# A fused language tower on one core: Gram products for two groups of four positions in column halves, two positions a transfer, later normalisers, first expert chunk inside the last step

## The chip, the cores and the metric

The kernel runs on one core of one Trainium2 chip. The metric is the device time of one execution in microseconds (us). The kernel before takes 741.24 us in the median of 3 runs (737.28 to 750.5). What can be told from no change is about 2% of that, 15 us.

## The reference

The input is 16 x 128 token numbers. The reference applies five blocks to a residual stream `h` of shape (16, 128, 64):

```python
h = L0_tok(x)                              # embedding, decaying memory, 4 MLP layers of 128 -> 512 -> 128, head to 64
h = h + L0_attn(layernorm(h))              # fast weights, described below
h = h + L0_ffn(layernorm(h))               # 8 experts 64 -> 128 -> 64, routed by the mean over 128 positions
h = h + L1_attn(layernorm(h))              # attention of 8 heads with positional scores
h = h + L1_ffn(layernorm(h))               # 8 experts, top 2 for each row
```

The change is in the second and third block. `L0_attn` runs over the first axis: 16 steps, for 128 positions and 8 heads of width 32, with a state of 32 x 32 per head:

```python
q, k = sum_norm(elu(q) + 1), sum_norm(elu(k) + 1);  rk = softmax(rk)
v_old = W @ k_t;   W = W + beta * (v_t - v_old) k_t^T;   z_t = W @ q_t
r_old = R @ rk_t;  R = R + rbeta * (rv_t - r_old) rk_t^T;  h_t = z_t + R @ softmax(h_{t-1})
out_t = x_t + concat(h_t) @ out_W^T
```

`L0_ffn` takes the mean of the normalised rows over the 128 positions of each of the 16 steps, two softmaxes of the router's logits with a capacity scale between them, the two largest weights, and the weighted sum of the experts.

## The kernel before, in words

Everything lies in the on-chip memory, with the 128 positions on the partitions; `t` is the step (T = 16), a chunk is CH = 4 steps, NC = 4 chunks.

**The Gram stage.** The kernel never builds the 32 x 32 states. It keeps for each step the updated value rows (`UV`), and needs inner products of every step's key or query with every earlier step's key. These are Gram products over (step, position), of which only those with equal position are wanted. The features stand transposed in `feat[0..5]` (32 rows for each of four heads on the 128 partitions). `grams(g)` takes a group of GB = 8 positions: for 8 heads and KD = 3 kinds one product of 16 x 8 = 128 columns of weights by 17 x 8 = 136 moving columns (the 17th step is a row of ones, whose products are the sums to divide by). There are NG = 16 groups; the heads of k = 0 go to banks 0 to 3, those of k = 1 to banks 4 to 7. ScalarE and VectorE copy two banks each of a half to a staging buffer (128 x 408 values a bank), of which there are NS = 4. Of each block of 8 x 8 positions only the diagonal is wanted. `relay(eng, g, j)` is a transfer from one place of the chip's memory to another: it reads 16 partitions (the 16 steps of position j of the group), 408 values each, and writes them side by side into the one partition `16 * j + g` of `C`. Three of a group's eight transfers are issued by the sync engine SP (lines 405 to 409), five by GpSimd (lines 574 to 579; of the last group two by ScalarE). Before a staging buffer is written again, `relayed` waits until its eight transfers have landed.

**Normalisers.** When all transfers have landed, VectorE's `row_sums` and `sums` (lines 1707 to 1722) invert the sums, make the strengths `bsum`, `bsum2` and scale the query coefficients, first for steps 0 to 3, then for steps 4 to 15, before `next_query(0)`.

**The steps.** `step(t)` on VectorE (line 1800) makes the softmax of the state, the read coefficients, the products of the `rec` kind, adds the output of step t - 1 to `H`, and then calls `next_query(t + 1)`, whose `update` gives GpSimd and TensorE what they need for the next step (`held`, `queries`, lines 493 to 520). TensorE (lines 1264 to 1275) sums and turns the products; ScalarE evicts (lines 825 to 834).

**The way out of the steps.** In step 15 VectorE makes the statistics and the normalised rows of chunks 0 to 2 (lines 1807 to 1812), with the inverse roots from GpSimd (`rstd_pool`, line 335); chunk 3 follows at lines 1902 to 1904. TensorE sums the columns (`means`), turns chunk 0 (`turn_x(0, 0)`), and the router's small softmaxes go to and fro between VectorE, ScalarE and TensorE (lines 1345 to 1361, 1939 to 1971), while ScalarE makes the Gelus of chunk 0 between the router's exponentials (lines 863 to 867). Then follow the bias products, `expert_up(0, 1)`, `turn_x(0, 2)` and the first `expert_down(0, 0)` (lines 1362 to 1370). VectorE's positional scores (lines 2005 to 2018) stand before its first addition of expert results (line 2024).

The order of the work on each engine is the order in which it is written; engines wait for each other by counted semaphores.

## Time and profile before

| what | value |
|---|---|
| median of 3 runs (lowest to highest) | 741.24 us (737.28 to 750.5) |
| the profiled execution | 740.56 us |
| its span | 738.7 us, 12304 instructions |
| busy: TensorE, its weight loads, VectorE | 606.3, 477.8, 445.8 us |
| busy: ScalarE, GpSimd | 280.9, 360.0 us |
| chain that ended last, by engine | PE 55%, DVE 26%, ACT 7%, DMA 4%, issue 4%, POOL 3% |
| DMA packets | 10699, 10.35 MB |
| DMA queue 0 (from GpSimd), queue 1 (from SP) | 2496 packets 2.04 MB, 7424 packets 7.12 MB |
| mean granted TensorE clock | 0.91 |

The profile is of one execution. Its page gives the busy time of each engine, the span in 40 equal slices, the DMA queues, the chain of waits that ended last, and the costliest groups of instructions by line. PE is TensorE, PEld its weight loads, DVE VectorE, ACT ScalarE, POOL GpSimd, SPq the sync engine's queue. A row `L1127 PE MATMUL bank<-features 32*128 32x136 f32 x768` is line 1127, weights of 32 rows by 128 columns, 136 moving columns, 768 times; an fp32 product is two such instructions. The square brackets of a timeline row hold the engine's idle time before it and what ended that.

### The profile page before, as it was taken

The page shows a single profiled execution, that of the slowest core. Times are in us where ns is not written, and L with a number is a line of the kernel's source. Part 1 is how long each engine was busy: PE and PEld are TensorE (multiplying, and loading weights), DVE is VectorE, ACT ScalarE, POOL GpSimd, SP SyncE. Part 2 cuts the span into 40 slices and gives each one's busy share as a digit, 9 for nine tenths or more (in the row PEclk, how much of TensorE's full clock was granted, in tenths as well). Part 3 has the DMA queues.
Part 4 walks back from the last instruction along what each step waited for, and adds up shares of the span by engine and source line. Part 5 has one row for each costly group of instructions (what it writes and reads, how often), then busy time and mean ns, then how long its engine had stood idle before and what let it go on. Part 6 is the DMA issues. An engine that isn't in the chain of part 4 may idle for free.

```text
span 738.7 us, 12304 instructions
## 1 busy us (share of the span) xinstructions
PE 606.3 (82%) x4657; PEld 477.8 (65%) x4657; DVE 445.8 (60%) x1113; ACT 280.9 (38%) x502; POOL 360.0 (49%) x414
## 2 busy tenths in 40 slices
PE   6889999999987707788877888456999698899996
PEld 3657777785556606677776777352678487785776
DVE  3643444236667756787899999952553736663533
ACT  0075453528966602111110000006553337566550
POOL 1696333218018836797899998143463300001334
PEclk9999999999989956888999999755999869999999
DMA  7000000000004450000000000000000000000000
GB/s 242 1 1 1 2 1 1 0 1 1 0 10 75 78 88 4 1 1 1 1 1 1 1 1 1 0 1 0 1 1 1 1 1 2 1 2 1 8 8 14
DMA packets 10699, 10.35 MB, mean 14 GB/s; under 512 B 5905, under 2 KB 9681, under 8 KB 10385
## 3 DMA queue, kind: packets, MB, share of 16 engines
q1 hardware_dynamic: 7424, 7.12, 3.6%
q0 software_dynamic: 2496, 2.04, 2.0%
q8 instruction: 37, 0.61, 0.4%
q10 hardware_dynamic: 720, 0.41, 0.3%
q14 instruction: 22, 0.17, 0.1%
HBM read 5.70 MB, written 0.52 MB: 8 GB/s over the span
## 4 chain that ended last, share of the span: by engine, by line
PE 55%; DVE 26%; ACT 7%; DMA 4%; issue 4%; POOL 3%; SPq 0%; ACTq 0%; DVEq 0%; POOLq 0%
PE bank L1059 8%; PE bank L1047 7%; DVE features L1743 6%; DVE bank L1777 5%; DVE features L1766 5%; PE bank L1315 4%; PE bank L1136 4%; PE bank L1333 4%; PE bank L1331 4%; PE bank L1403 2%; PE bank L1096 2%; PE bank L1391 2%; PE bank L1127 2%; PE bank L1105 2%; DMA RK<-in_wf 1%
## 5 line engine op out<-in xcount | busy, mean ns | idle before, releaser
L1136 PE MATMUL bank<-ident,features 128*128 128x128 f32 x920 | 126.9, 297 | 63.1 <-DVE features L1743 39.3
L1136 PEld LDWEIGHTS bank<-ident,features 128*128 128x128 f32 x920 | 113.8, 155 | 73.4 <-DVE features L1743 48.0
L506 POOL TENSOR_TENSOR features<-UV,coefs 128x1024 f32<-128x1024 f32 (+1 forms) x64 | 117.6, 1864 | 25.7 <-DVE UV L1730 12.5
L1743 DVE TENSOR_TENSOR features<-UV,bank 128x1024 f32<-128x1024 f32 (+3 forms) x64 | 66.2, 1066 | 0.9
L685 ACT ACTIVATE G<-bank,cols 128x512 f32<-128x512 f32 x64 | 43.3, 687 | 49.5 <-PE bank L1047 49.5
L1047 PE MATMUL bank<-xs,weights 128*128 128x512 f32 x128 | 60.2, 615 | 2.3 <-ACT xs L676 2.3
L1059 PE MATMUL bank<-weights,G 128*128 128x128 f32 x512 | 59.8, 275 | 0.0
L1059 PEld LDWEIGHTS bank<-weights,G 128*128 128x128 f32 x512 | 58.4, 192 | 0.0
L349 POOL TENSOR_SCALAR rstd<-mv 128x4 f32<-128x4 f32 x8 | 1.9, 238 | 112.2 <-DVE mv L361 112.2
L752 ACT ACTIVATE hsT<-bank 128x256 f32<-128x256 f32 x16 | 6.2, 385 | 102.3 <-PE bank L1136 102.3
L1127 PE MATMUL bank<-features 32*128 32x136 f32 x768 | 34.8, 320 | 10.5 <-DVE G L1703 4.1
L481 POOL TENSOR_TENSOR UV<-xs,rows 128x512 f32<-128x512 f32 x16 | 20.3, 1271 | 46.7 <-DVE xs L1652 46.6
L1766 DVE TENSOR_TENSOR features<-RK,bank 128x1024 f32<-128x1024 f32 (+3 forms) x40 | 41.8, 1044 | 0.1
L1047 PEld LDWEIGHTS bank<-xs,weights 128*128 128x128 f32 x128 | 24.0, 198 | 27.4 <-issue 24.5
L1777 DVE TENSOR_REDUCE bank<-features 128x32 f32<-128x1024 f32 (+3 forms) x40 | 41.5, 1056 | 0.0
L1127 PEld LDWEIGHTS bank<-features 32*128 32x128 f32 x768 | 29.7, 212 | 15.6 <-ACT G L736 4.6
L340 POOL TENSOR_SCALAR rstd<-mv 128x4 f32<-128x4 f32 x32 | 7.7, 241 | 61.8 <-DVE mv L361 60.6
L2065 DVE TENSOR_REDUCE RK<-bank 128x4 f32<-128x512 f32 x32 | 21.9, 684 | 26.0 <-PE bank L1391 26.0
L1652 DVE TENSOR_TENSOR xs<-bank,UV 128x512 f32<-128x512 f32 x16 | 11.1, 692 | 40.9 <-PE bank L1059 38.0
L342 POOL TENSOR_TENSOR rstd<-rstd,neghalf 128x4 f32<-128x4 f32 x32 | 33.2, 1038 | 2.7
L652 POOL TENSOR_TENSOR features<-features 128x512 f32<-128x512 f32 (+2 forms) x21 | 17.2, 818 | 27.1 <-DVE features L2158 17.1
L614 POOL TENSOR_TENSOR features<-weights,RK 128x512 f32<-128x512 f32 x16 | 16.4, 1043 | 28.0 <-PE bank L1331 15.6
(312 smaller groups left out, 1350.6 us busy)
## 6 DMA issues: line engine op xcount, KB each, us to landing
weights<-in_w SPq DMA_DIRECT2D x2, 1024.0 KB, 11.8
features<-in_tok SPq DMA_DIRECT2D x1, 768.0 KB, 6.3
weights<-in_ew SPq DMA_DIRECT2D x4, 128.0 KB, 3.0
weights<-in_ew SPq DMA_DIRECT2D x2, 256.0 KB, 2.9
coefs<-G POOLq DMA_DIRECT2D x20, 25.5 KB, 3.9
coefs<-xs POOLq DMA_DIRECT2D x20, 25.5 KB, 5.2
coefs<-weights POOLq DMA_DIRECT2D x20, 25.5 KB, 5.3
coefs<-sx POOLq DMA_DIRECT2D x18, 25.5 KB, 5.0
```

Of the source, the lines that this page charges most:

```text
L342: pool.tensor_tensor(rstd[:, k, 0:n], rstd[:, k, 0:n], neghalf[:, 0:n], ALU.pow).then_inc(s["ln_rstd"], 1)
L506: pool.tensor_tensor(out, u, co, ALU.mult).then_inc(s["held_p"], 1)
L685: act.activation(G[:, 4 * (w % 2) + f, :], up_bank(f)[:], ACT.Gelu, bias=col("b1", 4 * i + f)).then_inc(s["tok_gelu"], 1)
L1047: mm(up_bank(f)[:], w1[:, i, P * f:P * f + P], xT[:, w % 2, :], start=True, stop=True).then_inc(s["tok_up"], 1)
L1059: last = mm(down_bank(w)[:, DT * j:DT * j + DT], G[:, 4 * (w % 2) + f, P * j:P * j + P], w2[:, i, f, :], start=(f == 0), stop=(f == 3))
L1127: last = mm(bank[4 * k + j][:, GB * SL * n:GB * SL * n + GB * SL], feat[left + k][x, g, 0:T].rearrange("p s b -> p (s b)"), feat[right + k ...
L1136: last = mm(out[:, P * k:P * k + P], x[:, P * k:P * k + P], ident[:], is_transpose=True, start=first and k == 0, stop=last_ and k == n - 1 ...
L1315: mm(expert_bank(k, c, e)[:], ew1[k][r, e // 2, :], xin(k, c)[r], start=True, stop=True).then_inc(s[f"x_up{e % 2}"], 1)
L1331: last = mm(bank[4 + t % 2][:, 0:D], g, w2w[:, t % NW, e, :], start=(e == 0), stop=(e == E - 1))
L1743: dve.tensor_tensor(out, u, co.unsqueeze(3).broadcast_to([P, R, NH, DH]), ALU.mult)\
L1766: ch(dve.tensor_tensor(PD[:, j, 0:R * HB].rearrange("p (r x) -> p r x", r=R), RK[:, r0:r1_, :], e.unsqueeze(1).broadcast_to([P, R, HB]), A ...
L1777: ch(dve.tensor_reduce(bankCR[:, r0:r1_, :], PD[:, j, 0:(r1_ - r0) * HB].rearrange("p (r h j) -> p r h j", r=r1_ - r0, h=NH), AX_X, ALU.add))
```

## The change

Groups have 4 positions (GB = 4, NG = 32) and are treated in pairs: NR = 16 rounds. In a round each product of before becomes two, of 64 weight columns by 68 moving columns, one for each group of the pair, into partitions 0 to 63 and 64 to 127 of the same bank. A bank's copy has 204 values a partition in place of 408. There are NS = 6 staging buffers of half the size, in three of the four tensors used before. A transfer reads 32 partitions and writes two neighbouring partitions, `32 * j + 2 * g` and the next one: four transfers a round in place of eight, two from SP and two from GpSimd, none from ScalarE.

```diff
-GB = 8
+GB = 4
+NR = NG // 2
-NS = 4
+NS = 6
...
-            b = NG * j + g
-            eng.dma_start(CF[b:b + 1, 0:T * ROWC].rearrange("p (t x) -> p t x", t=T),
-                          stage[g % NS][j:P:GB, j].rearrange("p c s -> p (c s)"))\
+            b, x = NG * j + 2 * g, g % NS
+            eng.dma_start(CF[b:b + 2, 0:T * ROWC].rearrange("p (t x) -> p t x", t=T),
+                          stage[x][j:P:GB, j].rearrange("p c s -> p (c s)"))\
...
-            for g in range(NG):
+            for g in range(NR):
                 sp.wait_ge(s["gram_act"], 4 * g + 4)
                 sp.wait_ge(s["gram_dve"], 4 * g + 4)
-                for j in range(0, 3):
+                for j in (0, 1):
                     relay(sp, g, j)
...
-                            last = mm(bank[4 * k + j][:, GB * SL * n:GB * SL * n + GB * SL],
-                                      feat[left + k][x, g, 0:T].rearrange("p s b -> p (s b)"),
-                                      feat[right + k][x, g].rearrange("p s b -> p (s b)"), start=True, stop=True)
+                            for h in range(2):
+                                last = mm(bank[4 * k + j][D * h:D * h + D, GB * SL * n:GB * SL * n + GB * SL],
+                                          feat[left + k][x, 2 * g + h, 0:T].rearrange("p s b -> p (s b)"),
+                                          feat[right + k][x, 2 * g + h].rearrange("p s b -> p (s b)"), start=True, stop=True)
```

`sums` is split: before `next_query(0)` only steps 0 to 3 are inverted (`normalisers`), get their strengths and their query coefficients scaled, and of these only the columns in use. The rest goes into steps 0 to 4, and the first statistics and normalised rows into steps 5 and 8:

```diff
-                if t == T - 1:
-
-                    for c in range(NC - 1):
-                        norm_stats(dve, ch, ("f0", c), [H[:, i, :] for i in range(CH * c, CH * c + CH)])
-                    for c in range(NC - 1):
-                        x_apply(c)
                 if t:
                     out_add(t - 1)
+                if t == CH + 1:
+                    x_stats(0)
+                if t == 2 * CH:
+                    x_apply(0)
+                if t == 0:
+                    normalisers(slice(CH, T))
+                if t == 1:
+                    ch.settle()
+                    strengths(slice(CH, T))
+                if t >= 2 and t + 2 < 2 * CH - 1:
+                    query_scale(t - 1)
                 if t + 1 < T:
                     next_query(t + 1)
...
             for t in range(T):
                 step(t)
+            x_stats(1)
+            x_stats(2)
+            x_apply(1)
             out_add(T - 1)
-
+            dve.wait_ge(s["o_add"], T)
+            x_stats(NC - 1)
+            x_apply(2)
+            x_apply(NC - 1)
```

GpSimd makes the inverse root of chunk 0 before `held(7)`. TensorE turns chunk 0 and makes its eight up products inside step 15, with banks 4 and 5 for them, and ScalarE its Gelus there; chunk 1 takes the place of chunk 0 beside the router, and `turn_x(0, 2)` comes before the router's last product:

```diff
                 queries(t)
+                if t == T - 1:
+                    pe.wait_ge(s["load_experts"], 16 * 17)
+                    pe.wait_ge(s["pad"], 2)
+                    turn_x(0, 0)
+                    expert_up(0, 0)
                 read_out("rec", t, reads_of("rec", t))
...
+                if t == T - 1:
+                    experts(0, 0)
+                    expert_gelus(0, 0)
+                state(t)
+
+            experts(0, 1)
             act.wait_ge(s["mean_mm"], 1)
             act.activation(meanT[:], bank[7][0:D, 0:T], ACT.Copy, scale=1.0 / P).then_inc(s["mean_ready"], 1)
-            experts(0, 0)
             for j in range(3):
                 act.wait_ge(s["r_sub"], j + 1)
                 act.activation(rsel[0:T, j, :], rsel[0:T, j, :], ACT.Exp).then_inc(s["r_exp"], 1)
-                expert_gelus(0, 0, 2 * j, 2 * j + 2)
-            expert_gelus(0, 0, 6, E)
+            expert_gelus(0, 1, 0, 4)
             act.wait_ge(s["wT_mm"], 1)
             act.activation(wtsT[:], bank[7][:, 256:384], ACT.Copy).then_inc(s["wT_ready"], 1)
-            experts(0, 1)
+            expert_gelus(0, 1, 4, E)
+            experts(0, 2)
...
             pe.wait_ge(s["hs_saved"], T)
-            for c in range(NC - 1):
+            out_projection(T - 1)
+            means(0)
+            turn_x(0, 1)
+            for c in range(1, NC):
                 means(c)
-            out_projection(T - 1)
-            means(NC - 1)
+            expert_up(0, 1, 0, 2)
...
-            expert_up(0, 0, 0, 2)
+            pe.wait_ge(s["o_add"], T)
+            expert_up(0, 1, 2, 4)
             pe.wait_ge(s["r_prob"], 1)
...
-            expert_up(0, 0, 2, 6)
+            turn_x(0, 2)
             pe.wait_ge(s["r_spread"], 1)
...
-            turn_x(0, 1)
             bias(0)
+            expert_up(0, 1, 4, E)
```

## Rows read from the trace of the kernel before

**Rows 1.** Busy time by stretch: Gram stage, steps, way out to the expert chunks.

```profile
core 0: us, PE busy (x) PEld busy (x) DVE busy (x) ACT busy (x) POOL busy (x), PEclk, DMA share, GB/s
214.20:269.00 54.80, 34.78 (x768) 29.67 (x768) 33.38 (x65) 28.79 (x64) 37.65 (x78) 0.84 0.44 63
276.00:481.50 205.50, 155.09 (x1158) 139.93 (x1159) 176.83 (x252) 24.94 (x60) 162.21 (x108) 0.89 0.01 1
481.50:526.00 44.50, 29.57 (x134) 17.93 (x132) 21.46 (x104) 18.78 (x29) 16.75 (x20) 0.68 0.00 1
```

**Rows 2.** Groups by line in the Gram stage: busy us, mean ns, idle before.

```profile
L1703 DVE COPY xs<-bank 128x408 f32<-128x408 f32 x16 | 8.4, 577 | 3.9 <-PE bank L1127 2.3 <-DMA coefs<-xs 1.6
```

**Rows 3.** Timeline of SP's queue: the first two transfers.

```profile
218.54 1.18 SPq L379 DMA_DIRECT2D coefs<-G  x2
```

**Rows 4.** Busy time by stretch again: transfers in two fillings of queues, and weight loads.

```profile
224.00:226.00 2.00, 1.85 (x48) 1.48 (x48) 1.78 (x4) 1.44 (x4) 2.00 (x5) 1.00 0.58 92
...
262.00:264.00 2.00, 0.00 (x0) 0.00 (x0) 0.00 (x0) 0.00 (x0) 0.00 (x0) 0.50 1.06 72
272.00:282.00 10.00, 3.91 (x17) 3.15 (x17) 6.76 (x14) 1.07 (x3) 4.75 (x7) 0.50 0.34 89
```

**Rows 5.** The chain of waits in order of time: start, length, what.

```profile
221.34 6.55 DMA coefs<-G
...
261.94 6.92 DMA coefs<-sx
```

**Rows 6.** DMA queues and issues: packets, MB, share; KB, us to landing.

```profile
q0 software_dynamic: 2496, 2.04, 2.0%
...
cols<-in_cols SPq DMA_DIRECT2D x1, 0.5 KB, 2.4
```

**Rows 7.** Timeline of DVE after the last transfer.

```profile
270.98 1.95 DVE L1716 RECIPROCAL coefs<-coefs 128x288 f32<-128x288 f32 x1
...
273.78 1.75 DVE L1720 TENSOR_TENSOR coefs<-coefs 128x1536 f32<-128x1536 f32 x1
...
280.35 0.69 DVE L1730 TENSOR_TENSOR UV<-UV,bank 128x512 f32<-128x512 f32 x1 [2.14 <-PE bank L1156]
```

**Rows 8.** Timeline of POOL: the first product of the steps.

```profile
276.13 1.07 POOL L506 TENSOR_TENSOR features<-UV,coefs 128x512 f32<-128x512 f32 x1 [2.49 <-DVE smallv L1732]
```

**Rows 9.** Timeline of PE from the last step to the first expert sums.

```profile
478.13 6.06 PE L1136 MATMUL bank<-ident,features 128*128 128x128 f32 x32 [8.19 <-DVE features L1743]
...
495.26 1.02 PE L1280 MATMUL bank<-ones,sx 128*64 128x1 f32 x8 [5.41 <-DVE sx L373]
...
511.33 0.79 PE L1355 MATMUL bank<-RK,ones 16*128 16x128 f32 x2 [6.63 <-DVE RK L1968]
...
517.71 1.98 PE L1341 MATMUL bank<-features,RK 128*128 128x512 f32 x4 [0.37 <-ACT RK L869]
...
525.89 7.36 PE L1331 MATMUL bank<-features 128*128 128x64 f32 x64
```

**Rows 10.** Timeline of ACT: the last state.

```profile
484.23 0.39 ACT L752 ACTIVATE hsT<-bank 128x256 f32<-128x256 f32 x1 [17.89 <-PE bank L1136]
```

**Rows 11.** Groups of ACT by line, 496 to 527 us.

```profile
L856 ACT ACTIVATE features<-bank,cols 128x512 f32<-128x512 f32 x8 | 5.1, 685 | 3.1 <-PE bank L1315 3.1
...
L865 ACT ACT_TABLE_LOAD x2 | 2.6, 1283 | 0.0
```

**Rows 12.** Timeline of DVE on the way out of the steps.

```profile
481.39 0.60 DVE L358 BATCH_NORM_STATS2 stats<-H 128x6 f32<-128x64 f32 x4
...
486.75 0.98 DVE L373 TENSOR_SCALAR sx<-H,mv,rstd 128x64 f32<-128x64 f32 x4 [0.35 <-POOL rstd L342]
...
508.88 0.21 DVE L1911 TENSOR_TENSOR RK<-RK 16x64 f32<-16x64 f32 x1 [3.08 <-ACT RK L865]
...
520.46 0.17 DVE L2007 SCALAR_TENSOR_TENSOR gate<-rows 128x8 f32<-128x8 f32 x1
...
526.32 1.22 DVE L2018 TENSOR_TENSOR RK<-RK,comb 128x1024 f32<-128x1024 f32 x1
```

More of the change, by code:

```diff
@@ L326, in expert_bank @@
         def expert_bank(k, c, e):
+            if k == 0 and c == 0:
+                return bank[4 + e % 2]
             low, high = ((2, 0), (3, 1)) if k == 0 or c >= 2 else ((2, 4), (3, 5)) if c == 0 else ((2, 1), (3, 7))
@@ L588, in _ @@
                     pool.wait_ge(s["sums_done"], 2)
+                if t == 2 * CH - 1:
+                    rstd_pool(pool, ch, ("f0", 0), CH)
                 held(t)
@@ L595, in _ @@
             pool.wait_ge(s["masks"], 2)
-            for c in range(NC):
+            for c in range(1, NC):
                 rstd_pool(pool, ch, ("f0", c), CH)
-            pool.wait_ge(s["x_norm"], NC)
+            pool.wait_ge(s["hs_saved"], T)
             for k in range(2):
@@ L857, in expert_gelus @@
                                    bias=col(f"eb1{k}", e)).then_inc(s["x_gelu"], 1)
+            query_row(0)
+            held_out(1)
+            for t in range(T):
+                if t:
+                    exponentials(t)
+                if t + 1 < T:
+                    query_row(t + 1)
+                if t and t + 1 < T:
+                    held_out(t + 1)
+                if t == T - 1:
[3 more added lines that the diff above has]
+            experts(0, 1)
             act.wait_ge(s["mean_mm"], 1)
             act.activation(meanT[:], bank[7][0:D, 0:T], ACT.Copy, scale=1.0 / P).then_inc(s["mean_ready"], 1)
-            experts(0, 0)
             for j in range(3):
@@ L1241, in _ @@
             pe.wait_ge(s["rk_sub"], T)
-            for g in range(NG):
+            for g in range(NR):
                 grams(g)
-            pe.wait_ge(s["gram_act"], 4 * NG)
-            pe.wait_ge(s["gram_dve"], 4 * NG)
+            pe.wait_ge(s["gram_act"], 4 * NR)
+            pe.wait_ge(s["gram_dve"], 4 * NR)
             def queries(t):
@@ L1262, in second_half, with turn_x, expert_up @@
                 read_out("fast", t, part[len(part) // 2:])
+            tr = nc.tensor.transpose
+            def turn_x(k, c):
+                x = NC * k + c
+                if x >= 2:
+                    pe.wait_ge(s["x_xT"], x - 1)
+                if k == 0:
+                    pe.wait_ge(s["x_norm"], c + 1)
+                src = XN if k == 0 else YB[0]
+                for j in range(CH):
+                    tr(turn_bank(k, c)[0:D, P * j:P * j + P], src[:, CH * c + j, :], ident[:])
+                for j in range(CH):
+                    last = mm(turn_bank(k, c)[D:P, P * j:P * j + P], src[:, CH * c + j, :], ident[:], start=True, stop=True)
+                last.then_inc(s["x_T"], 1)
+            def expert_up(k, c, e0=0, e1_=E):
+                x = NC * k + c
+                pe.wait_ge(s["x_xT"], x + 1)
+                for e in range(e0, e1_):
+                    i = E * x + e
+                    if x == 0 and e >= 2:
+                        pe.wait_ge(s["x_gelu"], e - 1)
+                    elif x:
+                        pe.wait_ge(s["x_gelu"], i - 3)
+                    if k == 1 and c == 1 and e == 2:
+                        pe.wait_ge(s["pos_saved"], NC)
+                        pe.wait_ge(s["comb_done"], NC)
+                    r = slice(D * (e % 2), D * (e % 2) + D)
+                    mm(expert_bank(k, c, e)[:], ew1[k][r, e // 2, :], xin(k, c)[r],
+                       start=True, stop=True).then_inc(s[f"x_up{e % 2}"], 1)
             for t in range(T):
@@ L1786, in read_coefficients, with x_stats @@
                 ch.settle()
+            def x_stats(c):
+                norm_stats(dve, ch, ("f0", c), [H[:, t, :] for t in range(CH * c, CH * c + CH)])
             def x_apply(c):
@@ L1880, in _ @@
             ch(dve.reciprocal(beta[:], beta[:]))
-            for g in range(NG):
+            for g in range(NR):
                 grams(g)
-            dve.wait_ge(s["gram_act"], 4 * NG)
-            dve.wait_ge(s["gram_dve"], 4 * NG)
+            dve.wait_ge(s["gram_act"], 4 * NR)
+            dve.wait_ge(s["gram_dve"], 4 * NR)
             ch(dve.memset(bankER, 1.0))
             row_sums()
-            sums(CH, T)
             next_query(0)
@@ L1901, in _ @@
             dve.wait_ge(s["pad"], 1)
-            dve.wait_ge(s["o_add"], T)
-            norm_stats(dve, ch, ("f0", NC - 1), [H[:, t, :] for t in range(T - CH, T)])
-            x_apply(NC - 1)
             def rank2(x, sel, n, parts):
```

112 lines of the change are left out of this document (35 added, 77 removed).

## The prediction

> **What bounds the kernel now.** I first cut the span by stage. The Gram stage takes 54.8 us with TensorE busy for 34.78, VectorE 33.38, ScalarE 28.79 and GpSimd 37.65 [rows 1]: no engine fills it. The steps hold 205.5 us, mostly TensorE, VectorE and GpSimd by turns. In the way out of the steps, 44.5 us, nobody is busy for more than 29.57 and the granted clock is 0.68 [rows 1]: a chain of small steps. A copy of a bank waits on average for a product or a transfer [rows 2], so I looked at the transfers. The first is issued at 218.54 [rows 3]. The last link of the stage in the chain of waits is the transfer of 261.94 that lands 6.92 later, at 268.86, while the chain already held one of 6.55 us at 221.34 [rows 5]; an unloaded transfer takes 2.4 [rows 6]. The transfers end the stage, and the question is what their pace depends on. 128 of them, 16 x 1632 bytes each, are 3.34 MB; from 218.54 to 268.86, less 2.4, that is 70 GB/s.
>
> Three rows on the pace. The first burst makes 92 GB/s with engines 0.58 busy; with all queues full and TensorE, VectorE, ScalarE idle it is 72 GB/s at a share of 1.06; the expert weights, which go to many partitions, reach 89 GB/s at a share of only 0.34 [rows 4]. Transfers that write one partition each hold the engines about four times as long a byte: they stand in each other's way at the destination.
>
> **The Gram stage.** Bytes are unchanged. Half as many issues (64) and banks' copies of half the width, 0.577 [rows 2] going to about 0.36 by width with some 0.15 fixed, help engines that end nothing here. The first issue comes perhaps 0.4 us earlier, since the copies ahead of it are shorter: 218.1. What changes is the target: before, a round's eight transfers write eight separate partitions; now four transfers write pairs of neighbours, so at one time fewer, closer places are written. No row shows this. From below, five early transfers of GpSimd's queue (26.1 KB each) land together, in some 6.55 us, the length of the early link [rows 5]: 20 GB/s a queue, 41 for both. From above, 72 GB/s, the full queues of before, or 92, the best row [rows 4]. I take the middle of 41 and 72, 56.5 GB/s, as the new pattern is like the full one with fewer targets: 3.34 MB take 59.1 us, and the stage ends at 218.1 + 59.1 + 2.4 = 279.6, **+10.7**. The ends: 81.5 us (+33), 46.4 us (-2), 36.3 us (-12.1).
>
> The trace has a transfer's time a byte rising with crowded single-partition targets [rows 4]. The Trainium skill, "SBUF — State Buffer", section "Door 1: The DMA port swizzle", maps a partition to one of 16 ports by bits 2 to 4 and 6 of its number; by that a round's targets lie on 4 ports before and 2 after, and at its 27.2 GB/s a port the skill would give an estimate of 54.4 GB/s and 61.4 us, two more than my sum.
>
> **Normalisers.** Before, GpSimd's first product waits 2.49 us after the strengths, for the whole reciprocal and query scaling; it starts at 276.13, 5.15 after the reciprocal's start at 270.98 [rows 7, 8]. Now only a quarter of each stands ahead. I take 2.49 plus 0.5 for the smaller first pieces: **-3.0**. It is paid back inside the steps. The reciprocal of steps 4 to 15, 1.95, fits in VectorE's 2.14 of idle at 280.35 [rows 7], which hides it; uncovered it is 1.95. The later strengths cost 0.4 beyond an idle. The query scaling, 1.75 for 1536 elements [rows 7], returns in three pieces that sum to about 1.6. The statistics of chunk 0 cost 0.60 and their aggregate, 1.0, in step 5, the normalised rows 0.98 [rows 12] in step 8, on VectorE, which lies on the chain in each step. Behind each stands `next_query`, which holds up GpSimd and TensorE. GpSimd's inverse root, about 1.3 us ahead of `held(7)`, has slack: 0, at most 0.9. Together **+3.9** (2 to 6).
>
> **Step 15.** Eight transposing passes, eight up products, a copy and eight Gelus (5.1 us with 0.685 each, and a table load of 1.283 [rows 11]) stand before TensorE's last `rec` read-outs and ScalarE's last state. TensorE idles 8.19 us before its 6.06 of read-outs and ScalarE 17.89 before the last state [rows 9, 10]: at most 9.9 us of ScalarE work in 17.89, price **0**. If the up products, throttled by the Gelus that free their two banks, outlast TensorE's 8.19, the read-outs wait: +2.4. If the work keeps the clock up for read-outs now made at half of it: -1.7.
>
> **The way out.** Before, VectorE makes three chunks' statistics at 481.39 (0.60 and the aggregates), waits for GpSimd's roots, and only then applies (0.98 from 486.75 [rows 12]); `out_add(15)` and chunk 3 follow, and the mean's products end at 495.26 + 1.02 = 496.28 [rows 9], call it M. Now one chunk is gone, the output's addition stands ahead of all but one application, and the memsets stand behind: addition about 486, statistics 487, root and applications 489.4, means 490.4, **-5.9**.
>
> From M, before: the router's spread product at 511.33, M + 15.1, and the bias products at 517.71 with 1.98, M + 23.4; first expert sums at 525.89, M + 29.6 [rows 9]. A quarter of the sums is 1.84, so the third begins at 529.6, M + 33.3. Among it are waits for ScalarE, whose Gelus and table loads stand between the exponentials: 3.08 for the third alone [rows 12]. Now the three exponentials follow each other without Gelus: spread product at M + 9.9, weights M + 11.0. ScalarE then has a table load and four Gelus (1.28 + 2.5, from M + 7.9) ahead of the weights' copy: M + 11.7; bias done at M + 13.7. After it comes VectorE's base and its positional scores, 520.46 to 526.32 + 1.22, 7.1 us [rows 12]: M + 21.5. TensorE can make two quarters of sums sooner, but the third needs a bank that VectorE frees behind the scores: M + 21.7, **-11.6**, of which some 5 is the router, 4 the order after it. The way out gives 17.5 (12 to 19).
>
> **Sum.** +10.7 - 3.0 + 3.9 - 17.5 = -5.9, against the profiled execution's 740.56: **735.0 us** (734.7 exactly). That execution lies 0.7 under the median of 741.24. With the bounds above this case alone spans 722 to 757.
>
> **Rivals.**
> *A, above, 0.47.* About 2% is what a measurement of this kernel tells from no change, here below 726.4 and above 756. The pace of the transfers eats most of the gain.
>
> *B, targets don't matter, 0.33.* The 72 GB/s may be one queue's tail and the 1.06 share only transfers waiting behind each other; then TensorE and the copies, or the 92 GB/s [rows 4], set the pace. A round of TensorE is 34.78 / 16 = 2.2 us [rows 1], the copies 4 x 0.36 with their starts: 16 rounds in 36.3 us, end at 256.5, -12.4. With the rest, -16.6: -29.0, **711.5**. For it: the idle before a copy is more often TensorE's (3.9) than a transfer's (2.3) [rows 2]. Against it: the share of 1.06 with no other work.
>
> *C, slower: a transfer runs on few engines, 0.13.* A transfer of before has 16 rows written in one partition and its like fill all 16 engines (share 1.06 [rows 4]). The new one has an outer dimension of 2 at its target; if it is cut by that, two engines take 16 rows each. The queue of GpSimd held 2.0% of 16 x 738.7 = 236 us for its 78 transfers of 16 rows (2496 packets, two a row), 0.19 us a row [rows 6]; 16 rows are 3.0 us, and SP's 32 transfers on its two engines 97.3 us. End at 218.1 + 97.3 + 2.4 = 317.8, +49; less 16.6, +32: **773**. The 0.19 was measured in a crowd, so the price is likely lower: below 0.115 us a row this costs less than A does, and from 0.158 on the whole is slower by 2%.
>
> The Trainium skill, "DMA: Bandwidth & Descriptors", section "Why a DMA increments its semaphore by 16 and not by 1", states such a rule: the number of engines is the largest up to 16 that divides the slowest non-1 dimension of both sides, here 2. In the trace of before that dimension is 16 and all engines take part, which agrees but doesn't decide.
>
> *D, the way out gives half, 0.07.* Another wait takes the router's place, say ScalarE's Gelus of chunk 0 ending behind the state of step 15, or the weights' copy behind chunk 1's Gelus: -8 in place of -17.5, **744**.
>
> **Numbers.** Faster by over 2%: B, and a seventh of A: 0.33 + 0.07 = 0.40. Slower: C and a sliver of A, 0.16. Between: 0.44. The range reaches from below B's value, by its 7 us of uncertain terms, 704, to A's upper end, 757; C's upper part, and little of B's, is left out.
>
> **What would show it.** In the profile after: the bytes a second and the engines' share in the Gram stage, and the landing time of a transfer (A: 55 to 60 GB/s at a share near 1; B: over 85; C: packets on few engines, a low share, 40 GB/s or less); VectorE's first reciprocal at 281 (A), 258 (B), 318 (C); GpSimd's first product about 2.2 us after it; TensorE without a wait of its own between up products and last read-outs; from the end of these to the mean's product some 9 us, and from there to the third quarter of expert sums 21.7. Wrong it would be above all by the pace, of which no row shows the new pattern; next by steps in which the added pieces do not hide.

## The result and the profile after: 767 us, 3.8% slower

The changed kernel takes 767.24 us in the median of 4 runs (766.08 to 768.09), the one before 739.92 in the same runs: ratio 1.038, interval 1.035 to 1.042. The forecast was 735, the range 704 to 757. It ended on the side of rival C (773). C's mechanism, two engines a transfer, is at work in it, but costs this much only because the targets are crowded, as the experiments show.

The Gram stage in the trace after (busy time by stretch; clock, DMA share and GB/s last) answers to [rows 1, 4]:

```profile
core 0: us, PE busy (x) PEld busy (x) DVE busy (x) ACT busy (x) POOL busy (x), PEclk, DMA share, GB/s
217.60:300.70 83.10, 29.89 (x1416) 26.08 (x1406) 19.03 (x61) 16.72 (x61) 19.21 (x32) 0.50 0.27 43
...
222.00:230.00 8.00, 3.71 (x186) 3.16 (x177) 2.25 (x8) 2.43 (x9) 2.37 (x4) 0.50 0.48 50
...
290.00:300.70 10.70, 0.00 (x0) 0.00 (x0) 0.00 (x0) 0.08 (x1) 0.00 (x0) 0.50 0.11 26
```

83.1 us from the first issue to the first reciprocal, 50.6 before (218.54 to 269.18). No engine is busy for half of it, TensorE's clock is at the lower level of 1.2 GHz throughout, and in the last 10 us only transfers run, at a share of 0.11 of 16 engines, which is 1.8 engines. SP's queue says which. Its issues in time, the queues' totals over the span, and SP's queue in the stage alone (217.6 to 300.5):

```profile
217.62 2.98 SPq L381 DMA_DIRECT2D coefs<-G  x4
...
237.05 11.95 SPq L381 DMA_DIRECT2D coefs<-G  x4
```

```profile
q1 hardware_dynamic: 6976, 7.53, 3.6%
q0 software_dynamic: 3584, 1.70, 1.7%
q8 instruction: 43, 0.70, 0.4%
```

```profile
q1 hardware_dynamic: 1088, 1.67, 10.4%
```

The 1088 packets are SP's 32 transfers with 32 rows and 2 completions each, so I read a transfer as running on two engines. 10.4% of 16 engines' 82.9 us is 138 us: each of the two was held for 69 of 83 us, 0.13 us a row in the mean. Four issues that cost 2.98 us with room in the queue take 11.95 with none: 3.0 us a transfer there, 0.19 us for each of the 16 rows that one of two engines has to move. TensorE's line in the stage:

```profile
L1125 PE MATMUL bank<-features 32*64 32x68 f32 x1536 | 32.4, 329 | 30.1 <-issue 11.0 <-DVE weights L1707 8.8 <-DVE xs L1707 5.8
```

It stands 30 us, a third of it for "issue", nothing that the profile knows as a wait. The rest is for bank copies, which wait until a staging buffer's transfers have landed. From 250 us on TensorE makes one round (96 instructions) and stands for the copies again:

```profile
252.21 2.32 PE L1125 MATMUL bank<-features 32*64 32x68 f32 x96 [1.95 <-DVE weights L1707]
261.35 1.87 PE L1125 MATMUL bank<-features 32*64 32x68 f32 x96 [6.82 <-DVE weights L1707]
```

So in the changed kernel itself the transfers pace the second half of the stage. Then the steps and the way out, on GpSimd, VectorE and TensorE in order of time:

```profile
304.55 1.07 POOL L505 TENSOR_TENSOR features<-UV,coefs 128x512 f32<-128x512 f32 x1
...
352.09 0.23 POOL L342 TENSOR_SCALAR rstd<-mv 128x4 f32<-128x4 f32 x1 [7.27 <-DVE mv L363]
```

```profile
300.73 0.75 DVE L1723 RECIPROCAL coefs<-coefs 128x96 f32<-128x96 f32 x1 [18.92 <-DMA coefs<-xs]
...
390.14 5.96 DVE L375 TENSOR_SCALAR sx<-H,mv,rstd 128x64 f32<-128x64 f32 x4
...
525.39 4.12 DVE L375 TENSOR_SCALAR sx<-H,mv,rstd 128x64 f32<-128x64 f32 x4 [0.68 <-POOL rstd L344]
```

```profile
517.65 3.71 PE L1134 MATMUL bank<-ident,features 128*128 128x128 f32 x32
...
529.56 1.01 PE L1314 MATMUL bank<-ones,sx 128*64 128x1 f32 x8 [4.17 <-DVE sx L375]
...
540.15 0.79 PE L1362 MATMUL bank<-RK,ones 16*128 16x128 f32 x2 [3.38 <-DVE RK L1993]
...
542.17 3.74 PE L1350 MATMUL bank<-features,RK 128*128 128x512 f32 x4 [0.37 <-ACT RK L865]
...
547.75 3.79 PE L1340 MATMUL bank<-features 128*128 128x64 f32 x32
556.70 7.09 PE L1340 MATMUL bank<-features 128*128 128x64 f32 x32 [5.17 <-DVE xs L2049]
```

With the landmarks of before [rows 7 to 9, 12] the spans differ by 26.1 us (764.8 less 738.7), which splits so:

| stretch | before | after | change | forecast |
|---|---|---|---|---|
| up to the first reciprocal (269.18; 300.73) | 269.2 | 300.7 | +31.5 | +10.7 |
| from there to the first product of the steps | 6.95 | 3.82 | -3.1 | -3.0 |
| to the end of the last read-outs | 208.1 | 216.8 | +8.7 | +3.9 |
| to M, the end of the means | 12.1 | 9.2 | -2.9 | -5.9 |
| M to the third quarter of expert sums | 33.3 | 26.1 | -7.2 | -11.6 |
| the rest | 209.1 | 208.1 | -1.0 | 0 |

### The profile page after: what moved, and what is told of

It reads as the page before. It is cut to its first block, busy times and chain, and to the rows that moved or that the text cites. A ratio compares the mean times of both kernels' runs of the same rounds, so it can differ in the third digit from the quotient of the medians.

```text
span 764.8 us, 13760 instructions
## 1 busy us (share of the span) xinstructions
PE 603.9 (79%) x5425; PEld 473.0 (62%) x5425; DVE 442.4 (58%) x1115; ACT 267.4 (35%) x500; POOL 341.0 (45%) x368
## 3 DMA queue, kind: packets, MB, share of 16 engines
q1 hardware_dynamic: 6976, 7.53, 3.6%
## 4 chain that ended last, share of the span: by engine, by line
PE 28%; DVE 18%; ACT 4%; issue 2%; POOL 0%; DVEq 0%; ACTq 0%
PE bank L1290 4%; DVE features L1758 4%; PE bank L1134 4%; PE bank L1342 4%; PE bank L1340 4%; DVE bank L1792 3%; DVE features L1781 3%; PE bank L1409 2%; PE bank L1397 2%; DVE sx L375 1%; PE bank L1432 1%; PE bank L1469 1%; PE bank L1421 1%; PE bank L1274 1%; ACT UV L929 1%
## 5 line engine op out<-in xcount | busy, mean ns | idle before, releaser
L1134 PEld LDWEIGHTS bank<-ident,features 128*128 128x128 f32 x920 | 110.5, 152 | 84.4 <-DVE features L1758 40.3
L505 POOL TENSOR_TENSOR features<-UV,coefs 128x1024 f32<-128x1024 f32 (+1 forms) x64 | 117.3, 1860 | 22.9 <-DVE UV L1745 11.6
L1125 PE MATMUL bank<-features 32*64 32x68 f32 x1536 | 32.4, 329 | 30.1 <-issue 11.0
L1125 PEld LDWEIGHTS bank<-features 32*64 32x64 f32 x1536 | 28.5, 207 | 34.1 <-issue 14.3
L616 POOL TENSOR_TENSOR features<-weights,RK 128x512 f32<-128x512 f32 x16 | 16.6, 1053 | 28.5 <-PE bank L1340 17.8
```

The costliest lines, as they stand in the source:

```text
L505: pool.tensor_tensor(out, u, co, ALU.mult).then_inc(s["held_p"], 1)
L1125: last = mm(bank[4 * k + j][D * h:D * h + D, GB * SL * n:GB * SL * n + GB * SL], feat[left + k][x, 2 * g + h, 0:T].rearrange("p s b -> p ( ...
L1134: last = mm(out[:, P * k:P * k + P], x[:, P * k:P * k + P], ident[:], is_transpose=True, start=first and k == 0, stop=last_ and k == n - 1 ...
```

## Experiments on the Gram stage

The theory at this point was rival C, two engines a transfer, against forecast A's mechanism, neighbouring targets. All times of a stage below are from SP's first issue to the first reciprocal.

**e1_one_target** cuts each transfer in two, of 16 rows and one partition.

```diff
-            eng.dma_start(CF[b:b + 2, ...], stage[x][j:P:GB, j])
+            for h in range(2):
+                eng.dma_start(CF[b + h:b + h + 1, ...], stage[x][D * h + j:D * h + D:GB, j])
```

> The changed kernel, each transfer of 32 rows into two neighbouring partitions cut into two of 16 rows into one partition; targets, bytes, order and queues stay, 128 issues in place of 64. Few-engines theory (a transfer with an outer dimension of 2 runs on two engines): the Gram stage ends again after 42 to 55 us instead of 83, the first reciprocal starts at 260 to 273 instead of 300.7, the time is 727 to 740. Neighbouring-targets theory (the pairs of neighbours stand in each other's way): the same partitions are written at the same time, so the stage stays at 75 us or more and the time above 758.

771.53 us, ratio 1.042 (1.037 to 1.047), stage 85.3. The queues show 7936 packets for SP in place of 6976: 64 transfers with 16 completions in place of 32 with 2, which bears the two engines out, and doing away with them gained nothing by itself. First burst and TensorE:

```profile
222.00:230.00 8.00, 2.52 (x126) 2.17 (x127) 1.94 (x6) 1.73 (x6) 2.73 (x6) 0.50 1.12 54
```

```profile
L1126 PE MATMUL bank<-features 32*64 32x68 f32 x1536 | 32.9, 329 | 46.5 <-issue 46.1
```

All 16 engines are held (1.12) for 54 GB/s; in the same stretch the kernel before moves 82 at 0.65. The transfers have the same rows; what differs is their targets and TensorE's doubled instructions. The rival's "75 us or more" is what came. But e1 is slow in another way than the changed kernel: TensorE never waits for a copy here, and nearly all of its 46.5 us are "issue". So e1 does not clear the two engines of the changed kernel's 83.1.

**e2_before_two** was to put two engines on the kernel before.

```diff
-            eng.dma_start(CF[b:b + 1, 0:T * ROWC].rearrange("p (t x) -> p t x", t=T),
+            eng.dma_start(CF[b:b + 1, 0:T * ROWC].rearrange("p (t x) -> p t x", t=2),
```

> The kernel before, with only the target's shape of each transfer written as 1 x 2 x 3264 in place of 1 x 16 x 408; targets, bytes, issues and order stay. Few-engines theory: SP's 48 transfers take 8 rows on each of two engines, 48 x 8 x 0.16 = 61 us in place of 50, and two completions a transfer are seen instead of sixteen; the time is 745 to 765, more if GpSimd's five transfers a group also gather on few engines. Neighbouring-targets theory: nothing changes, 740.

739.02 us, ratio 0.997 (0.994 to 1.000), but SP's queue has the same 7424 packets as before: sixteen completions a transfer. The edit did not change what it was to change, and the run tells nothing of engines.

**g1_before_halves** and **g2_after_short** are about the "issue" time. The trace of e1 shows where it falls: TensorE stops after Gram product instruction 221, 347, 474, 601, 727, 854, 981, 1107, 1234, 1361 and 1488, 126 or 127 apart (254 instructions with their weight loads), and each stop begins within 1.6 us of the start of a packet of 16384 bytes on the queue that the page calls "instruction". For three of them:

```
packet 223.27, took 3.39    TensorE stands from 224.57 for 8.42
packet 234.55, took 1.28    TensorE stands from 235.74 for 1.94
packet 246.15, took 3.26    TensorE stands from 246.06 for 7.83
```

The reading that fits is that TensorE has used up its block of code and stands until the next has come. The change doubled its instructions in the stage: 12 such packets between SP's first issue and the first reciprocal, 6 before. In the changed kernel this shows in the first half alone, four stops of 1.5 to 3.2 us at such places.

```diff
 g1: before.py, grams
-                            last = mm(bank[...][:, 136 columns], left, right)
+                            for h in range(2):
+                                last = mm(bank[...][:, 68 columns of half h], left, right half h)
 g2: after.py, relay
-            CF[b:b + 2, ...] "p t x", stage[x][j:P:GB, j]
+            CF[b:b + 2, ...] "p t x" [:, :, 0:64], stage[x][j:P:GB, j][:, 0:64]
```

> The kernel before with each Gram product cut into two of half the moving columns (68 in place of 136): 1536 matmul and 1536 weight-load instructions in place of 768 and 768, the same results, copies, transfers and targets. Instruction-supply theory (with the instructions doubled TensorE uses up each 16 KB block of code in some 3 us and then stands until the next block, which queues on the DMA engines behind the transfers): gaps of 1 to 8 us every 127 matmuls, the stage 20 to 32 us longer, 760 to 772. Rival (the transfers, their shape or their targets alone set the changed kernel's stage; the weights are only loaded once more, hidden beside the copies): at most 5 us more, 740 to 745.

772.83 us, ratio 1.044 (1.034 to 1.054): the number came, the mechanism did not.

```profile
218.00:303.00 85.00, 76.88 (x1442) 76.68 (x1438) 33.55 (x64) 28.79 (x63) 37.52 (x78) 0.50 0.16 42
```

TensorE is busy for 77 of 85 us (a stage of 83.7), at the lower clock, with no stop over 1 us: 128 columns of weights loaded twice, for half the moving columns each time, fill the stage by themselves. A forecast that hits by a cause it did not name is no support for it. It also sets a limit to the reading: with the same 43 packets of code over the span, TensorE, which takes over 6 us for 127 products here and 2.8 in e1, never stood for one.

> The changed kernel with each transfer cut from 408 to 64 values a row (same number of rows, issues, targets and waits; the rest of the coefficients is left at ones, so the later stages compute something else). Instruction-supply theory: with little in front of them the code blocks arrive in 1 us, and TensorE's gaps nearly vanish; the two-engine queue of SP also drains, if its price is by the byte. The stage falls from 83 to 40 to 55 us. Rival for SP's queue (a price by the row, not by the byte): SP's issues still take some 3 us apiece in the full stretch and the stage stays over 70.

One run: 734.21 us, stage 47.8 in place of 83.1 (a fill of the coefficients with ones was put ahead of the stage); SP's issues take 0.75 to 1.2 us, so the price is by the byte.

```profile
L1131 PE MATMUL bank<-features 32*64 32x68 f32 x1441 | 31.4, 329 | 16.5 <-issue 11.3 <-DVE G L1713 3.6 <-DVE xs L1713 1.2
```

The stops stay, nearly one a block, which the theory did not expect, but are 1.1 us each in place of e1's 4.2. TensorE's stand for "issue" is 11 us even with light transfers in front of it, and the transfers decide how much more; how much of it the stage's end feels no run isolates.

**h1_spread16, h2_spread2** change the targets alone, with sixteen and with two engines a transfer; **h3_sp_one** relieves SP.

```diff
 h1, h2: groups g and g + 16 in place of 2g and 2g + 1
-  feat[left + k][x, 2 * g + h, 0:T]      b = NG * j + 2 * g
+  feat[left + k][x, g + NR * h, 0:T]     b = NG * j + g     (h2: CF[b:b + NR + 1:NR, ...])
 h3: transfers of a round
-  sp: j in (0, 1)    pool: j in (2, 3)
+  sp: j in (0,)      pool: j in (1, 2, 3)
```

> The kernel with one-partition transfers (e1_one_target), but a round's two groups are g and g + 16 in place of 2g and 2g + 1: its targets are 32j + g and 32j + g + 16, eight scattered partitions a round as in the kernel before; instructions, bytes, issues and queues as in e1. Target theory (neighbouring targets at one time make the transfers slow, and they hold up the code blocks): the share of the DMA engines falls from 1.1 to 0.5 in the first burst at 75 us or GB/s or more, TensorE's gaps shrink from 46 us to some 15 to 25, the stage from 85 to 55 to 65, the time 740 to 752. Instruction-supply theory alone (doubled code is slow whatever the targets): gaps and stage stay, 765 to 775.

> The changed kernel, two partitions a transfer, but the two are 16 apart (groups g and g + 16), so only the targets differ; each transfer still completes twice, on two engines. Few-engines theory (SP's 32 transfers on two engines are what ends the changed kernel's stage): the targets hardly matter, SP's issues still take about 3 us apiece, stage 75 to 85 us, time 758 to 768. Target theory: stage 55 to 65, time 738 to 750.

> The changed kernel with one of a round's four transfers from SP and three from GpSimd in place of two and two. Few-engines theory (SP's queue always works on the same two engines, GpSimd's transfers go round all of them): SP's queue is no longer the last, the stage falls to 60 to 72 us, 742 to 755. Rival (code blocks or targets set the pace, not SP's queue): stage within 3 us of 83, 764 to 770.

h1: 745.42 us, ratio 1.005 (1.001 to 1.008), stage 62.2. h2: 737.12, ratio 0.994 (0.991 to 0.998), stage 55.1. h3: 754.86, ratio 1.020 (1.014 to 1.027), stage 68.4. The first burst of h2:

```profile
222.00:230.00 8.00, 4.48 (x223) 3.90 (x208) 2.61 (x9) 2.30 (x8) 2.37 (x4) 0.50 0.30 77
```

77 GB/s at 0.30, where the changed kernel has 50 at 0.48. SP's queue in h2's stage (216.8 to 271.6):

```profile
q1 hardware_dynamic: 1088, 1.67, 9.1%
```

The same packets hold its two engines for 80 us together in place of 138, 0.08 us a row in place of 0.13. Nothing but the targets differs between the two kernels, so this shows the cause. The clock is not it either: it is 0.50 in both. Of the 2 x 2, the targets are worth 28.0 us with two engines and 23.1 with sixteen; the edit to sixteen engines, which also doubles the issues, costs 2.2 and 7.1 us. So with good targets the few engines cost less than that edit. With bad ones they are part of it: h3, with all its targets as bad, gains 14.7 us from a lighter SP queue, and both its stage and its time came within what the few-engines theory expected (60 to 72 us, 742 to 755).

**i1_two_apart, i2_four_pair** ask what is bad in a target: the two of a transfer lie 2 or 4 apart.

```diff
-  feat[left + k][x, g + NR * h, 0:T]                      CF[b:b + NR + 1:NR, ...]
+  i1: feat[left + k][x, 4 * (g // 2) + g % 2 + 2 * h, 0:T]   CF[b:b + 3:2, ...]
+  i2: feat[left + k][x, 8 * (g // 4) + g % 4 + 4 * h, 0:T]   CF[b:b + 5:4, ...]
```

> The changed kernel with the two targets of a transfer two partitions apart (4m and 4m + 2, or 4m + 1 and 4m + 3), not neighbours but in the same aligned block of four. Port theory (partitions with the same bits 2 to 4 and 6 share one way in; the Trainium skill, SBUF — State Buffer, Door 1: The DMA port swizzle): as slow as the changed kernel, stage 75 to 88 us, 760 to 772. Adjacency theory (only direct neighbours hurt, say by a shared row of the memory): as h2_spread2, stage near 54, 735 to 742.

> The same with the two targets four apart (p and p + 4, in the next block of four). Port theory: a round has its targets on four ports in place of two, as with 16 apart; stage 52 to 60 us, 735 to 745. Distance theory (close targets hurt, the less the farther apart): between the changed kernel and h2_spread2, stage 62 to 75, 747 to 760.

i1: 770.79 us, ratio 1.043 (1.038 to 1.048), stage 86.8. i2: 737.24, ratio 0.997 (0.994 to 0.999), stage 51.0. Bursts of i1 and of i2:

```profile
222.00:230.00 8.00, 2.69 (x127) 2.32 (x127) 1.29 (x4) 1.73 (x6) 1.18 (x2) 0.60 0.53 40
```

```profile
222.00:230.00 8.00, 5.36 (x254) 4.79 (x253) 2.88 (x10) 2.71 (x10) 2.17 (x4) 0.50 0.26 71
```

Two apart is as bad as neighbours; four apart is as good as sixteen. Adjacency is out, and so is a loss that fades with distance. What fits is the aligned block of four; a limit at a distance of four would fit these two runs as well, as no run puts targets one to three apart over a block's edge. The Trainium skill ("SBUF — State Buffer", section "Door 1: The DMA port swizzle") says so: blocks of four partitions with equal bits 2 to 4 and 6 share a port. By that rule a round has its targets on two ports in the changed kernel, e1 and i1, and on four before and in h1, h2 and i2; the runs agree in their order, and e1's 54 GB/s with all engines held lies at 54.4, an estimate from the 27.2 that the section gives a port. It is no cap on longer stretches: h3, also on two ports a round, moves 66 GB/s from 240 to 250 us, perhaps because several rounds are in flight.

**i3_four_apart** uses it on the kernel before: positions of a group 4 apart, eight ports.

```diff
-  ... "p (t b g) -> p t g b", g=NG            b = NG * j + g
+  ... "p (t y b z) -> p t y z b", y=4, z=4    b = 32 * (g // 4) + 4 * j + g % 4
```

> The kernel before, but the eight positions of a group are 4 apart (32(g/4) + 4j + g mod 4) in place of 16 apart: the same instructions, transfers and bytes, eight targets on eight ports in place of four. Port theory: the transfers' pace rises from 70 GB/s towards 90 or more, the stage falls from 50.7 us (first issue to first reciprocal) to 38 to 45, the time by 5 to 12 us, 728 to 735. Rival (four ports already suffice, and TensorE, the copies or the issues set the pace): within 3 us of the kernel before.

735.62 us, ratio 0.996 (0.993 to 1.000), stage 44.9 in place of 50.6.

```profile
218.00:262.00 44.00, 30.13 (x733) 24.79 (x728) 32.66 (x64) 28.39 (x63) 37.45 (x78) 0.97 0.37 79
```

79 GB/s in place of 69 at a lower share (0.37, before 0.47), though the targets now lie closer than before. GpSimd is busy issuing for 37 of 44 us; likely its five issues a group now set the pace. The stage is 5.7 us shorter in the trace; the median fell by 5.1, but the ratio's interval ends at 1.000, so the time alone doesn't decide between the port theory (5 to 12 us) and its rival (within 3).

## Experiments on the rest of the change

**e3_root_later** moves one call on GpSimd.

```diff
-                if t == 2 * CH - 1:
+                if t == 2 * CH + 1:
                     rstd_pool(pool, ch, ("f0", 0), CH)
```

> The changed kernel with GpSimd's inverse root of chunk 0 before held(9) in place of held(7), which it reaches when VectorE is past the statistics. Queue theory (GpSimd runs over a step ahead and stood 7.27 us in the wait for VectorE's statistics): 6 to 9 us less, 758 to 761. Rival (steps are set by VectorE, which spends 1.0 us on the statistics and 5.9 on the normalised rows; GpSimd makes its wait up): within 2 us of 767.

765.08 us, ratio 1.032 (1.026 to 1.038; changed kernel 1.038). By the trace `held(7)` begins right after the queries of step 5 (346.25 after 345.21 + 1.08), without the 7.27 us of standing; from the first product of the steps to M it takes 222.3 us in place of 226.0. So 3.7 us, not 6 to 9: of 8.5 us that GpSimd gained at that point, over half was waited for elsewhere later. The median is 2.2 us below the changed kernel's, and the two intervals overlap: by the time the rival (within 2 us) is nearer, by the trace it lies between the two.

**e4_apply_stt** and **g4_rest_mended** are about VectorE's normalised rows, 1.5 us apiece in step 8 instead of 0.24.

```diff
-    last = dve.tensor_scalar(o, x, mean, rstd, subtract, mult)                    # before, after: 4 x 64
+    e4: dve.scalar_tensor_tensor(in0=x, scalar=mean, in1=rstd repeated, ...)      # 4 x 64
+    g4: tensor_tensor(o, x, mean repeated, subtract); tensor_tensor(o, o, rstd repeated, mult)   # 2 x 256
```

> The changed kernel with the normalised rows of the second block made by the two-tensor form (row minus mean, times the root as a repeated second operand) in place of the form with two scalars, which took 1.47 us apiece beside a GpSimd product and 0.24 alone. Held-by-GpSimd theory (that form alone has to wait for GpSimd's running product): the four of step 8 take about 1 us instead of 5.9, the last chunk's about 1 instead of 4.1, and the time falls by 3 to 7 us. Rival (any VectorE operation of this size is slowed beside GpSimd, or something else holds it): durations and time stay within 1 us.

769.14 us, ratio 1.039 (1.034 to 1.044): the four rows of step 8 take 5.12 us, those of the last chunk 4.10. The form is not the cause.

**g3_gram_undone** is the changed kernel with the Gram stage of before.

> The changed kernel with its Gram stage (groups, staging buffers, transfers) as before; normalisers, steps and way out as changed. By the landmarks of the changed kernel's trace the rest is worth -3.1 (start of the steps), +8.8 (steps), -2.9, -7.2 and -1.0 (way out): 735. If the blind sum of the rest (-16.6) were right and the steps only suffered from the late stage, 724. If the rest gains nothing, 740.

740.57 us, ratio 1.000 (0.997 to 1.004). The rest of the change is worth nothing that can be measured: from the first reciprocal to the end its trace has 467.5 us, the kernel before 469.5, and its stage, the same code, was 53.4 in place of 50.6 in the profiled execution. The 735 that the landmarks of the changed kernel promised did not come.

> As the one before it, with the inverse root of chunk 0 before held(9) and the normalised rows made by two plain tensor-tensor operations of 256 values, in place of four with a scalar operand a partition. Scalar-operand theory (VectorE operations that take their scalars from memory are slowed beside GpSimd's products, those with tensors alone are not): the rows take about 0.75 us in step 8 and on the way out, 5 to 8 us less than the one before it, 727 to 730. Rival (everything VectorE does there is slowed): 3 to 4 us less from the root alone, 731 to 732.

734.58 us, ratio 0.994 (0.990 to 0.997). The two operations of g4, first alone, then beside GpSimd's `b2x`:

```profile
483.77 0.43 DVE L1824 TENSOR_TENSOR sx<-H,mv 128x256 f32<-128x256 f32 x1 [0.74 <-POOL rstd L345]
...
491.14 2.05 DVE L1824 TENSOR_TENSOR sx<-H,mv 128x256 f32<-128x256 f32 x1 [1.00 <-POOL rstd L345]
493.22 2.01 DVE L1827 TENSOR_TENSOR sx<-sx,rstd 128x256 f32<-128x256 f32 x1
```

0.43 us alone, 2.05 and 2.01 beside products of 1.9. The scalar operand is not the cause either, though the time fell by 6.0 us from g3, as the theory of it had forecast (5 to 8): the number hit without its mechanism. The root's move (2.2 to 3.7 by e3) explains a part, and the rows of step 8 take 3.9 in place of 5.96; the rest is not isolated. The step's own products of 1024 elements, one factor of which is in a matmul bank, take 1.13 to 1.22 beside the same GpSimd work. The Trainium skill ("SBUF — State Buffer", section "Who interferes with whom") states what fits all these rows: a VectorE instruction with two inputs in that memory, and a GpSimd instruction that reads it exclude each other for the whole instruction, and a VectorE instruction in a two-port mode excludes any of GpSimd's. Both rewritten forms have two such inputs. That `tensor_scalar` ran in such a mode no run shows.

**h4_best**, built on g4, takes `b2x` away from the rows and puts the first additions between the positional scores; **i4_best** adds the placing of i3.

```diff
+            pool.wait_ge(s["x_norm"], NC)
             for k in range(2):
                 pool.tensor_tensor(b2x[:, k], ...)
-            pool.wait_ge(s["x_norm"], NC)
...
             for h in range(NH): tensor_scalar(plog[:, h, :], ...)
+            add_experts(range(0, 2))
             for h in range(NH): scalar_tensor_tensor(plog[:, h, :], ...)
+            add_experts(range(2, CH))
```

> g4_rest_mended (Gram stage of before, rest of the change mended), with GpSimd's products b2x after the normalised rows as in the kernel before, and VectorE's additions of the first four expert sums put between the positional scores (two after the first eight operations, two after the next). If the rows of the last chunk are slow only beside b2x, 3 us less; if TensorE stood 5.1 us for the third sum and lost its clock by that (two quarters in 7.1 us in place of 3.7), 5 to 8 us less: 723 to 727. Rival (the additions only move the wait behind the scores, into the softmax): 730 to 734.

> h4_best with the same placing of the groups. Port theory: 5 to 12 us less than h4_best's 731, 719 to 726. Rival: 729 to 733.

h4: 731.39 us, ratio 0.986 (0.980 to 0.993), 3.2 us below g4. That is the rival's range (730 to 734), not the 723 to 727 of the theory. i4: 723.31, ratio 0.978 (0.971 to 0.985), within its port theory's 719 to 726 and the fastest of all, though not clear of 2%. In h4:

```profile
488.10 0.43 DVE L1823 TENSOR_TENSOR sx<-H,mv 128x256 f32<-128x256 f32 x1 [1.00 <-POOL rstd L345]
```

```profile
507.05 7.36 PE L1348 MATMUL bank<-features 128*128 128x64 f32 x64
```

The same rows take 0.43 with `b2x` behind them, and the four quarters of expert sums run through at the full clock, 7.36 us, where the changed kernel needed 3.79, a stand of 5.17 and 7.09. But a wait has moved, as the rival said, if to another place: TensorE now stands for ScalarE's Gelus and goes on at the lower clock,

```profile
520.75 4.36 PE L1298 MATMUL bank<-sx,weights 64*128 64x512 f32 x8 [4.42 <-ACT features L847]
```

and from the first sums to the next set it is 19.8 us (507.05 to 526.87), in the changed kernel 23.2, before 13.8.

## Why the prediction was wrong

- **The Gram stage (+10.7; measured +31.5)** is the step that failed: the term takes one pace of the transfers, 56.5 GB/s, as the pace of the whole stage, 3.34 MB in 59.1 us. That targets stand in each other's way was right (h2, i2), and so was the pace for a burst: 54 GB/s in e1's, 50 in the changed kernel's. But the stage made 43. The sum had no term for SP's queue, whose 32 transfers keep two engines held for 83% of the stage, while TensorE stands for the copies behind them and the last 10 us make 26 GB/s; relieving that queue alone gives back 14.7 us (h3). It also leaves TensorE out where it says that issues and copies "help engines that end nothing here": I counted half as many issues and never the 768 more matmuls with their 768 loads, and TensorE stood 11 us for "issue", most of it at the ends of blocks of code. How the missing 21 us divide between these no run shows.
- **Rival C (0.13, 773)** had the queue's mechanism right and was put too low; its signs came nearer than A's (a share of 0.27, 43 GB/s). That its time is nearly right is in part luck: it took the price of a row as given. Its 0.19 us was measured in SP's full queue, but is itself a product of the crowded ports: the mean over the stage is 0.13, and in h2, on two engines as well, 0.08. A transfer takes SP's full queue 3.0 us here, while in h2 four issues never take more than 6.22, 1.6 each. The whole stage came to +31.5, not C's +49, and C's time comes out near because it took 16.6 us off for the rest, of which 5.5 came in this trace.
- **Rival B** asks for a stage end at 256.5 and -12.4; its own terms, 218.1 + 36.3 + 2.4, give 256.8 and the -12.1 of the bounds. Nothing hangs on it.
- **Start of the steps (-3.0; -3.1)** right.
- **Steps (+3.9; +8.7).** GpSimd's root was priced at 1.3 us with slack. The instruction is that long; the wait ahead of it, for VectorE's statistics of step 5, was not priced, though GpSimd is ahead there and stood 7.27 us. e3's trace puts 3.7 us on it, its median 2.2. The rows of step 8 were priced at 0.98 from a row without GpSimd beside them, and took 5.96; how much of that reached the end no run isolates. Whether the reciprocal and the scalings hide no run isolates.
- **Step 15 (0, bounds -1.7 to +2.4).** Both bounds came about: the read-outs start right behind the throttled up products, some 3 us after the first of VectorE's products that they sum is done, and take 3.71 us in place of 6.06. They nearly cancel.
- **To M (-5.9; -2.9).** The missing 3 us are the last rows, 4.12 in place of 0.98, beside `b2x`; in h4 they are gone, and the stretch is 5.8 us in place of 9.2.
- **From M (-11.6; -7.2).** The router was right: its spread product at M + 9.6, forecast 9.9. Then the bias products took 3.74 at a clock of 0.53, which fell while TensorE stood for the router, and the positional scores 9.9 us in place of 7.1, beside GpSimd's seven products for the weights. The stand for the third quarter cost a second time: the clock fell again, and from that quarter to the second set of sums after it (583.36; before 552.15) it was 26.7 us in place of 22.6. That second cost had no term. The way out gave 10.1 of 17.5 up to the third quarter, 6.0 with the second cost taken off, near rival D's 8 though not by the waits that D named. For all behind the Gram stage the forecast was -16.6; this trace has -5.5, and g3's median shows nothing.

What stays open: how the 28 us of the targets divide between SP's slow queue and late code, since crowded targets worsen both; and why e1's stops of 8 us outlast the code block's own packet of 3.4.

## What to carry to other kernels

For transfers inside the chip's memory count the ports of the partitions written at one time, not the bytes: targets in different aligned blocks of four (h2, i2) took 28 to 32 us off the stage, with only the numbering of the groups changed. Count also how many engines one queue's transfers can use, as a slow port and a narrow queue multiply. Price a doubled count of short instructions by its code blocks where the engine runs through a block faster than one arrives, and every wait put into a queue by how far that queue runs ahead. When the rows that price an operation come from a stretch where its neighbour engine is idle, they are a lower bound.

## What the runs showed of the hardware that was not expected

- TensorE stops after each 126 or 127 short matmuls with their weight loads, each time beside one packet of 16384 bytes of the instruction queue (e1): 1.1 us a block with light transfers (g2), up to 8.4 with crowded ones (e1), none over 1 us where it takes over 6 us a block (g1).
- Targets 1 or 2 partitions apart: 40 to 54 GB/s; 4 or 16 apart: 71 to 77 in the same stretch (222 to 230 us). SP's rows cost 0.13 us apiece on crowded ports and 0.08 on others (changed kernel, h2).
- By the packets of SP's queue a transfer into two partitions completes twice, one into a single partition with 16 rows sixteen times, also where the target was written as 1 x 2 x 3264 (e2).
- VectorE operations with both inputs in the same memory last as long as GpSimd's running product, 2.0 us in place of 0.43.
